# A first attention whose turned outputs are copied by ScalarE, inverted by VectorE and multiplied by GpSimd, with GpSimd's splits reordered

## What is computed

```python
def _L0_attn_ref(x, W_qkv):
    qkv = x @ W_qkv
    q, k, v = jnp.split(qkv, 3, axis=-1)
    ...
    scores = jnp.einsum('bhnd,bhmd->bhnm', q, k) / jnp.sqrt(jnp.float32(D_MODEL))
    attn = jax.nn.softmax(scores, axis=-1)
    out = jnp.einsum('bhnm,bhmd->bhnd', attn, v)
    ...
x = L0_attn_x
x = _layernorm(x + _L0_attn_ref(x, L0_attn_W_qkv), axis=-1)
```

## Time and profile before

| | |
|---|---|
| median of 3 runs | 1023.99 us |
| the profiled execution | 1023.77 us |
| its span in the trace | 1021.7 us |
| busy: PE, DVE, ACT, POOL | 979.9, 826.8, 732.8, 523.6 us |
| one batch of the first attention, steady | 41.75 us |

### The profile page before, as it was taken

The page is one execution under the profiler, slowest core; times in us unless marked ns, Lnnn a source line. Parts: engine busy times, 40 slices in busy tenths (PEclk is TensorE's granted clock), DMA queues, the critical chain, the costliest instruction groups (busy, mean ns, idle before and its releaser), DMA issues. The chain is left out here.

```text
span 1021.7 us, 20122 instructions
## 1 busy us (share of the span) xinstructions
PE 979.9 (96%) x5769; PEld 469.4 (46%) x5769; DVE 826.8 (81%) x1811; ACT 732.8 (72%) x945; POOL 523.6 (51%) x631
## 2 busy tenths in 40 slices
PE   8999999999999999999999999999999999999996
PEld 4422222222222246888888887863232333222585
DVE  7999999999999867889788789987666666644677
ACT  4377887878888776655555555668889888999753
POOL 3051744726538745677677676675443144310275
PEclk9999999999999999999999999999999999999999
DMA  7661223122130005323433432443422332230011
GB/s 229 205 226 48 81 64 109 45 87 95 40 109 17 3 4 165 122 87 127 143 99 95 154 115 80 151 147 98 150 87 68 92 123 73 66 108 1 1 32 52
DMA packets 73548, 97.04 MB, mean 95 GB/s; under 512 B 12620, under 2 KB 42188, under 8 KB 73100
## 3 DMA queue, kind: packets, MB, share of 16 engines
q1 hardware_dynamic: 73496, 96.40, 29.7%
HBM read 68.18 MB, written 27.79 MB: 94 GB/s over the span
## 5 line engine op out<-in xcount | busy, mean ns | idle before, releaser
L780 DVE TENSOR_REDUCE a_nmax<-a_ps_f 128x1 f32<-128x512 f32 x512 | 319.7, 683 | 7.7 <-PE a_ps_f L627 5.3
L542 ACT ACTIVATE a_prob<-a_ps_s 128x1024 f32<-128x1024 f32 x256 | 250.0, 1022 | 63.5 <-PE a_ps_s L683 62.3
L1428 ACT ACTIVATE a_prob<-a_ps_s 128x1024 f32<-128x1024 f32 x256 | 244.4, 1026 | 27.8 <-PE a_ps_s L1480 26.8
L2248 POOL TENSOR_TENSOR moe_hl<-moe_hid,moe_hh 128x512 fp32r<-128x512 f32 x134 | 174.2, 1305 | 84.1 <-ACT moe_hh L2129 84.0
L627 PE MATMUL a_ps_f<-a_ks,a_qs 48*128 48x512 bf16 x512 | 156.9, 384 | 10.7 <-DVE a_nmax L780 3.1
L2119 ACT ACTIVATE moe_ps<-moe_ps 128x512 f32<-128x512 f32 x128 | 74.5, 582 | 111.6 <-PE moe_ps L2042 110.8
L1493 PE MATMUL a_ps_o<-a_prob,a_va 128*32 128x512 f32 x1024 | 136.4, 605 | 1.8 <-DVE a_turned_o L1608 1.2
L696 PE MATMUL a_ps_o<-a_prob,a_va 128*32 128x512 f32 x1024 | 136.4, 605 | 0.5 <-ACT a_prob L542 0.4
L683 PE MATMUL a_ps_s<-a_qs,a_ks 51*128 51x512 bf16 x512 | 131.8, 381 | 1.7 <-ACT a_prob L542 1.4
L627 PEld LDWEIGHTS a_ps_f<-a_ks,a_qs 48*128 48x128 bf16 x512 | 38.5, 93 | 193.9 <-DVE a_nmax L780 188.1
L2170 DVE TENSOR_TENSOR moe_prod<-moe_cw,moe_ps 128x512 f32<-128x512 f32 x128 | 87.3, 682 | 27.4 <-PE moe_ps L2042 26.7
(11 more groups left out here) (324 smaller groups left out, 1636.1 us busy)
## 6 DMA issues: line engine op xcount, KB each, us to landing
moe_cw<-r_weights SPq DMA_DIRECT2D x256, 128.0 KB, 2.8
parts_q<-a_parts SPq DMA_DIRECT2D x48, 256.0 KB, 2.5
parts_k<-a_parts SPq DMA_DIRECT2D x48, 256.0 KB, 2.6
a_qs<-parts_q SPq DMA_DIRECT2D x126, 96.0 KB, 2.4
a_ks<-parts_k SPq DMA_DIRECT2D x126, 96.0 KB, 2.4
out_x<-g_X SPq DMA_DIRECT2D x7, 256.0 KB, 2.3
a_prob<-in_x_t SPq DMA_DIRECT2D x3, 512.0 KB, 5.4
moe_wg<-in_wg SPq DMA_DIRECT2D x1, 1088.0 KB, 6.7
```

Of the source, the lines that this page charges most:

```text
L542: nc.scalar.activation(prob[:, u % PSLOTS, :, :], ps_s[:, u % 2, :, :], ACT.Exp, scale=float(P) ** -0.5).then_inc(exp_done, 1)
L780: nc.vector.tensor_reduce(nmax[:, half_no, h % 2, col:col + 1], ps_f[:, bank, :], AX.X, ALU.max, negate=True).then_inc(max_done, 1)
L1428: nc.scalar.activation(prob[:, u % PSLOTS, :, :], ps_s[:, u % 2, :, :], ACT.Sigmoid, scale=float(HD) ** -0.5).then_inc(exp_done, 1)
L2248: nc.gpsimd.tensor_tensor(hl[:, part_at(j), :], hid[:, hid_at(j), :], hh[:, part_at(j), :], ALU.subtract).then_inc(hl_done, 1)
```

## The change

ScalarE gets a copy of each turned output from its PSUM bank to SBUF (`take_turned`, 128x512, into a new tile `turned_o`). The bank is free when that copy is done (`o_copied`), no longer when the division is. VectorE no longer divides at o0 and o1; it computes the reciprocal alone, from SBUF, four turns later (`invert`, ahead of turns 50 and 13). GpSimd does the two multiplications (`divide`, L877 of the new file). In GpSimd's queue the `split_max` for max0 now stands ahead of `split_qk`, and the multiplication of o0 between the splits of q and k. In SyncE's queue `parts_to_dram` moves behind the `max_rows` of max0. The last batch keeps the old way, and so does turn o1 in it. That makes 13 moved divisions: o0 of batches 0 to 6, and o1 for the outputs of batches 0 to 5.

```diff
-                if qk_on:
-                    parts_to_dram(b + 2, p)
                 if fore:
                     max_rows(b + 1, 1 - p, 0)
                 if qk_on:
+                    parts_to_dram(b + 2, p)
...
+            def take_turned(b, n):
+
+                act.wait_ge(att_done, NO * b + n + ATT_C)
+                take(turned_o[:, :], ps_f[:, BANK[f"o{n}"], :], ot_done, NO * b + n + 1 + OT_C, o_copied)
+
...
+                            if back and t == "o0" and not is_last(b):
+                                take_turned(b, 0)
+                            if tail and t == "o1" and not is_last(b):
+                                take_turned(b - 1, 1)
...
-                    pe.wait_ge(att_done, NO * (b - 1) + (int(t[1]) + 1) % NO + ATT_C)
+                    count = NO * (b - 1) + (int(t[1]) + 1) % NO
+                    if is_last(b - 1):
+                        pe.wait_ge(att_done, count + ATT_C)
+                    else:
+                        pe.wait_ge(o_copied, count)
...
+            def invert(b, n):
+
+                dve.wait_ge(o_copied, NO * b + n + 1)
+                dve.wait_ge(att_done, NO * b + n + ATT_C)
+                nc.vector.reciprocal(rec[:, :, :, :], output_parts(turned_o[:, :])[:, :, :, :, HD]).then_inc(rec_done, 1)
...
+            def divide(b, n):
+
+                o, to = output_parts(turned_o[:, :]), outputs_of(att, n)
+                pool.wait_ge(rec_done, NO * b + n + 1)
+                for q in range(PER_O):
+                    ins = nc.gpsimd.tensor_tensor(to[:, :, :, q, :], o[:, :, :, q, 0:HD],
+                                                  rec[:, :, :, q].unsqueeze(3).broadcast_to([P, NT, HG, HD]), ALU.mult)
+                ins.then_inc(att_done, 1)
...
                 if u0 == 0 and tail:
+                    if not is_last(b):
+                        divide(b - 1, 1)
                     add_x(b - 1)
                     normalise(b - 1)
-                if u1 == NU and qk_on:
+                if u1 == NU and qk_on and not back:
...
+                    if qk_on and back:
+                        split_qk(b + 2, 0)
+                    if back:
+                        divide(b, 0)
+                    if qk_on and back:
+                        split_qk(b + 2, 1)
```

More of the change, by code:

```diff
@@ L67 @@
 STATS_AT = 16
+REC_AT = (50, 13)
 LOOP_U = 11
@@ L350, in attention0 @@
         sel = sel.rearrange("p (n a j m) -> p n a j m", n=2, a=PARTS, j=PLACED)
+        turned_o = sb("turned_o", [P, T])
         pool_gate, qk_gate = sb("pool_gate", [P, 1]), sb("qk_gate", [P, 4])
@@ L378, in attention0 @@
             sem(n) for n in ("o_taken", "ot_done", "rec_done", "att_done", "sum_done", "norm_step"))
+        o_copied = sem("o_copied")
         S2_C, EXP_C, PV_C, O_C, OT_C, ATT_C = NU, 2, PSLOTS // 2, 1, 2, 1
@@ L798, in units @@
                         for t in turns_of(u, second):
-                            if back and t == "o0":
+                            if back and t == "o0" and is_last(b):
                                 divide(b, 0)
-                            if tail and t == "o1":
+                            if tail and t == "o1" and is_last(b):
                                 divide(b - 1, 1)
+                            if back and t == REC_AT[0] and not is_last(b):
+                                invert(b, 0)
+                            if tail and t == REC_AT[1] and not is_last(b):
+                                invert(b - 1, 1)
                             if isinstance(t, int) and (back if t < LATE else fore):
```

## The result

| | before | after |
|---|---|---|
| median | 1024.06 us (6 runs, 1023.93 to 1026.32) | 1031.07 us (6 runs, 1030.52 to 1034.16) |
| the profiled execution | 1023.77 us | 1031.09 us |
| its span | 1021.7 us | 1029.2 us |
| steady batch, from turn 11 to turn 11 | 41.7 us | 42.1 to 41.9 us (the first, from batch 0 to batch 1: 42.8) |

The changed kernel takes 1.0071 times as long, 95% interval 1.006 to 1.0081, so 6.1 to 8.3 us more. 1030.3 was forecast, between 1026 and 1034.5.

What follows compares the result with a forecast made beforehand. The prediction took TensorE's chain to bound the kernel at the divisions, which lie in a gap on VectorE. Terms 3.8 + 2.2 + 0.3 = 6.3 us on 1023.77 gave 1030.1, stated as 1030.3, range 1026 to 1034.5.

Steps and rivals of the forecast that it cites:

- The bound: At o0 and o1, TensorE's chain sets when turns 47 and 11 come; taking the divisions off VectorE gains 0.
- The reciprocals: On VectorE ahead of turns 13 and 50: each costs 0.29 us, 13 cost 3.8 us; bounds 1.4 and 4.6.
- the reciprocals are made good: Rival: reciprocals fall into a lead of TensorE, so only 2.2 + 0.3 us remain, 1026.5 us; chance 0.08.
- ScalarE's copies: Copies of 0.60 us at o0 and o1 end before turns 47 and 11 load: cost 0; uncovered 7.8 us.
- The chain to q and k: From split of k to turn 8's load: group 0.2 us late, queue takes in some 0.35, cost 0.
- The multiplications: On GpSimd at o0 and o1: 0.46 us each, 0.9 for two; upper bound 0.73 each, 1.45 for two.
- Batch 6: GpSimd's full queue there: `add_x` 3.6 us late, TensorE waits 2.2 us for `split_max`, and nothing gives it back.
- the sum: Reciprocals 3.8, batch 6 2.2 and into batch 7 0.3 us, 6.3 us in all; every other part 0.
- Into batch 7: GpSimd's weight pieces end at 352.0, the maxima are ready at 351.7: cost 0.3 us.
- those for "right": Idle 0.8 us ahead of turns 11 and 47, batches 0.6 us longer, batch 6 wait over 2 us, copies in time.
- those for "wrong": Reductions 0.622 us apart through o0 and o1, or TensorE waiting for DMA or `turned_o` at turn 8, max1 or 47.

Runs made afterwards that it cites:

- the maxima earlier: Changed kernel with GpSimd's last split of the maxima (max0) of batch 6 one weight piece earlier: 1027.45 us, ratio 1.0034.
- the split of k first: Changed kernel with GpSimd's multiplication of o0 behind the split of k, not between q and k: 1029.5 us, ratio 1.0046.
- the run without divisions: Kernel before, with two one-element fills in place of each division of o0 and o1 but the very last: 1023.64 us, ratio 1.0001.
- the one without reciprocals: Changed kernel with a one-element fill in place of each of the 13 moved reciprocals: 1028.64 us, ratio 1.0052.
- the new order alone: Kernel before with only the new order in the queues of GpSimd and SyncE, division still on VectorE: 1023.63 us, ratio 1.0.
- all three mended: Changed kernel with batch 6's maxima split earlier, o0's multiplication behind the split of k, reciprocals ahead of turns 47 and 11: 1024.24 us, ratio 1.0004.

## Why the prediction was right, and where it was not

**The bound.** Right, and the main step: the divisions lay in a gap of TensorE's making. Without them the time is the same (1023.64), and 0.77 to 0.79 us of idle time stands where they were.

**The reciprocals: 3.8 forecast, 1.4 measured.** The failed step is "VectorE's next four reductions follow without slack, so what VectorE loses there is kept". The reciprocal itself is nearly as forecast (0.344 us long; 0.26 to the next start, where I had 0.29). But my 0.622 us between reductions was a mean over 36 steps; three of four are 0.60, the fourth 0.68. The 0.09 between them is a wait for TensorE, which the mean spread over all. The loop of TensorE and VectorE sets the pace, and VectorE has 0.09 us of room in every four turns. With the shorter reduction behind it, that makes good 0.155 of each reciprocal's 0.26 us. So the rival "the reciprocals are made good" was true by more than half.

**Where the reciprocal reads from.** The Trainium skill (VectorE: DVE Perf Modes, "The TRN2 errata") gives a lower fixed cost from SBUF. The runs don't show it: 0.344 us from SBUF here, 0.35 from PSUM.

**ScalarE's copies: 0 forecast, 0.2 measured.** Right in all batches but one. In batch 2 the copy runs from 167.21 to 167.82, and turn 47 loads at 167.94 without a wait of its own. In batch 1 the copy ends at 125.99, TensorE waits 0.29 us for it, and turn 47 comes 0.2 us late. The forecast had only 0.1 us between copy and load, and read it from one batch.

**The chain to q and k: 0 forecast, 1.3 measured.** I found the group 0.2 us late with 0.35 to be taken in, and rested it on one batch's SyncE times. In five batches that held within 0.2 us: turn 8 waited for the DMA, and the gap ahead of turn 11 took in all or most of it. In batch 1 SyncE took 0.8 us longer from write to read, and 1.05 us were lost. The multiplications, which I named as the weakest number, were on the good side: 0.41 us each, 0.79 the pair. The Trainium skill (GPSIMD Engine Reference, "Engine selection") calls such work about twice as slow there; against VectorE's pair of 0.49 it is 1.6 times.

**Batch 6: 2.2 forecast, 2.4 measured.** Right in place and size. What I left out is its consequence, 1.0 us of lower clock; the sum has no term for it.

**Into batch 7: 0.3 forecast, nothing measured.** GpSimd's pieces took up nearly all of its 4.33 us of waiting, but 0.66 us are left at 355.65, since the lower clock had made the maxima 1.0 us later. By the forecast the pieces would have been the later of the two by 0.3 us; without the lower clock that is what these numbers give too.

**The signs that the prediction named.** Of those for "right", the idle 0.8 us ahead of turn 47 and the wait in batch 6 came; ahead of turn 11 it was 0.48, with 0.21 ahead of turn 9; and a batch took 0.2 to 0.4 us more, not 0.6. One of those for "wrong" came as well: TensorE waited for a DMA at turn 8 in all six batches, and once for `turned_o`.

So the 6.3 us of the sum met 6.3 us at the last reduction, but by errors that cancel: 2.4 too much at the reciprocals and 0.3 at batch 7, against 1.3, 1.0 and 0.2 not counted and 0.2 too little at batch 6. That the sum came out is luck. The experiments hold the terms apart: 3.2 us for batch 6 with its clock (the maxima earlier), 1.3 for k (the split of k first), 1.4 for the reciprocals (none). What the remaining 1.0 us outside the attention's reductions comes from was not tested; in the traces of the experiments the part ahead of the first reduction differs from before by -0.2 to 0.3 us, and the part behind the last by -0.1 to 0.9.

## What to carry to other kernels

Before work is taken off the busiest engine, ask whether the instruction behind it could start earlier; replacing the work by an empty one, as in the run without divisions, answers this in one run. A mean over a merged row hides short waits: look at the single starts, since steps of 0.60, 0.61, 0.60, 0.68 say that one reduction in four waits for another engine, and that there is a little room. When a queue is reordered, follow the chain behind it in the first round as well as in a steady one, and count what a stop of some us does to TensorE's clock behind it.

## What the runs showed of the hardware that was not expected

In three kernels here (the changed one, the one without reciprocals and the one with the split of k first) TensorE waited 2.25 to 2.38 us in batch 6, between stretches at full clock. In each its granted clock fell to a half, the 1.2 GHz level, 0.8 to 2.1 us after it had gone on, and stayed there for some 3.4 us. The other seven traces have neither such a wait there nor such a fall. The fall cost 1.0 us in the changed kernel and 1.2 to 1.3 in the two others, about half of the wait once more.

A stop is not all that stands ahead of a fall. In the profiled executions of the new order alone and of all three mended, the clock fell to a half at 55 us for 10.2 and 6.8 us. TensorE had been busy 4.61 of the 5 us before, as in the changed kernel, where it did not fall there. What set it off is not shown.

The Trainium skill (TensorE: Matmul & The Clock Gate, "What's actually happening") tells of a gate that activity opens and idleness closes between these two levels. The three falls behind a stop agree with it, and add that the fall came only when the work ran again; the two at 55 us do not show it.
